# Slots 6 to 29 of a gated cross-attention block in another order: outputs turned by DMA, projection one slot later, tokens' low part on GpSimd

## The reference

```python
x = x + jnp.tanh(g_xattn[0]) * _L0_xattn_ref(_layernorm(x, axis=-1), ctx_768, mask, Wq, Wk, Wv, Wo)
x = x + jnp.tanh(g_ffn[0]) * _L0_ffn_ref(_layernorm(x, axis=-1), clip_x, clip_down, w_gate, w_up, w_down)
```

## Time and profile before

| | |
|---|---|
| median of 3 runs | 621.61 us (620.71 to 624.11) |
| the profiled execution | 621.71 us, span 619.9 us |
| busy in the span | PE 600.6, DVE 517.4, ACT 376.0, POOL 235.2 us |
| granted TensorE clock, mean | 0.991 |

### The profile page before, as it was taken

How to read it: one execution, slowest core, us unless ns; L and a number is a source line. 1 busy time by engine, 2 the same in 40 slices (tenths; PEclk the granted TensorE clock), 3 DMA queues, 4 the chain that set the end, 5 groups by cost and what they waited for, 6 DMA issues and landing times. The chain is left out here.

```text
span 619.9 us, 12094 instructions
## 1 busy us (share of the span) xinstructions
PE 600.6 (97%) x3706; PEld 448.7 (72%) x3727; DVE 517.4 (83%) x957; ACT 376.0 (61%) x484; POOL 235.2 (38%) x473
## 2 busy tenths in 40 slices
PE   8999999999999999999999886999999999899997
PEld 6799999999999999999899873444444444444544
DVE  6788899999999998999889857888888888866765
ACT  5554677877777777777774435555555553455653
POOL 6253454545454454445333112111011110067775
PEclk9999999999999999999999997999999999899999
DMA  8534885463434444634642000396653110199633
GB/s 310 174 116 121 197 192 106 82 112 80 109 81 100 89 92 92 126 81 91 124 103 59 16 1 10 75 252 226 205 158 87 35 34 1 45 369 396 242 117 120
DMA packets 118507, 77.89 MB, mean 126 GB/s; under 512 B 98211, under 2 KB 100669, under 8 KB 118461
## 3 DMA queue, kind: packets, MB, share of 16 engines
q1 hardware_dynamic: 113169, 60.51, 38.4%
q10 hardware_dynamic: 5292, 16.82, 7.6%
HBM read 32.48 MB, written 21.36 MB: 87 GB/s over the span
## 5 line engine op out<-in xcount | busy, mean ns | idle before, releaser
L1452 ACT ACTIVATE sb_silu<-ps_g,sb_sgu 128x512 f32<-128x512 f32 x88 | 60.5, 687 | 72.1 <-PE ps_g L1547 43.5
L1547 PE MATMUL ps_g<-sb_xqT,sb_wgu 128*128 128x512 bf16 x344 | 89.3, 379 | 1.0 <-DVE sb_xqT L1503 0.6
L1547 PE MATMUL ps_u<-sb_xqT,sb_wgu 128*128 128x512 bf16 x346 | 89.4, 379 | 0.3
L1518 DVE SCALAR_TENSOR_TENSOR sb_h<-ps_u,sb_sgu,sb_silu 128x512 f32<-128x512 f32 (+1 forms) x88 | 66.1, 751 | 19.8 <-PE ps_u L1547 18.9
L1069 PE MATMUL ps_q<-sb_xT_hi,sb_wq_hi 128*128 128x256 f32 x256 | 75.3, 294 | 0.9 <-DVE sb_xT_lo L764 0.6
L632 ACT ACTIVATE sb_prob<-sb_prob 128x616 f32<-128x616 f32 x64 | 45.6, 713 | 46.5 <-DVE sb_prob L797 46.5
L1628 POOL TENSOR_TENSOR sb_wgu<-sb_wgu,sb_x 128x512 f32<-128x512 f32 x31 | 53.3, 1721 | 53.7 <-DVE sb_wgu L1685 53.4
L1071 PE MATMUL ps_q<-sb_xT_hi,sb_wq_lo 128*128 128x256 f32 x256 | 72.4, 283 | 0.0
L1070 PE MATMUL ps_q<-sb_xT_lo,sb_wq_hi 128*128 128x256 f32 x256 | 72.3, 283 | 0.0
L1752 PE MATMUL ps_z<-sb_wdT,sb_hq 128*128 128x512 bf16 x324 | 71.3, 379 | 0.3
L1522 DVE TENSOR_REDUCE sb_hmax<-sb_h 128x1 f32<-128x512 f32 (+1 forms) x88 | 60.4, 686 | 7.6
(11 more groups left out here) (238 smaller groups left out, 1426.2 us busy)
## 6 DMA issues: line engine op xcount, KB each, us to landing
h_spill<-sb_h SPq DMA_DIRECT2D x4, 2816.0 KB, 9.5
sb_h<-h_spill ACTq DMA_DIRECT2D x16, 704.0 KB, 6.6
out_dram<-sb_wgu SPq DMA_DIRECT2D x31, 256.0 KB, 2.2
sb_x<-in_x_dram ACTq DMA_DIRECT2D x5, 1024.0 KB, 6.6
sb_w_in<-in_L_ffn_w_gate_dram SPq DMA_DIRECT2D x11, 256.0 KB, 2.7
sb_w_in<-in_L_ffn_w_up_dram SPq DMA_DIRECT2D x11, 256.0 KB, 2.6
sb_x<-in_x_dram SPq DMA_DIRECT2D x2, 1024.0 KB, 14.6
sb_x<-in_x_dram SPq DMA_DIRECT2D x2, 512.0 KB, 4.7
```

What stands on the lines that cost most here:

```text
L1452: act.activation(silu[(j * KI + i) % 2][:, :, :].rearrange("p t n -> p (t n)"), p_g[(j * KI + i) % 2][:, :], ACT.Silu, scale=sgu[:, i:i + ...
L1518: dve.scalar_tensor_tensor(steps_h, p_u[(j * KI + i) % 2][:, :, :], sgu[:, KI + i:KI + i + 1], silu[(j * KI + i) % 2][:, :, :], ALU.mult, ...
L1547: last = pe.matmul(banks[(j * KI + i) % 2][:, :], wgu[:, what, k, i * P:(i + 1) * P], xqT[j][:, k, :], start=(k == 0), stop=(k == KD - 1))
```

## The change

In slots 6 to 29 (`lagging`) and, for the parts that trail, 7 to 30 (`lagged`), each engine gets an order of its own:

- The outputs of tiles 4 to 27 are transposed by DMA. DVE writes `o_sb` as before, POOL splits it into planes (`out_split`, into the same buffer as the probabilities' planes), SP transposes back into `o_sb` (`outs_transposed`), ACT joins the planes (1024 half words) and casts the high part, DVE subtracts for the low part from the joined copy. `out_transpose` is gone for these tiles.
- TensorE projects tile n-3 right behind the first scores of tile n, and `outputs(n-1)` stands last in the slot.
- The low part of the tokens is computed by POOL (`x_low`), for tile n+3 in slot n. ACT's join of the tokens moves to the start of the slot, for tile n+3.
- DVE scales the second half of the outputs one slot later, and takes the weight rows' maximum and rounding at other places.
- `prob_transposed(n)` also waits for `out_part(n-2)`. Some semaphores are merged (t_ck into t_c) or renamed.

```diff
+LAG0 = 6
+OUT0, OUT1 = LAG0 - 2, NT - 4
...
+                o_u = o_sb[:, :].bitcast(U16)
+                o_pairs = o_u.rearrange("p (n two) -> p two n", two=2)
+                o_planes = o_u.rearrange("p (two n) -> p two n", two=2)
+                opl_planes = ppl_u[:, 0, 0:2 * D].rearrange("p (two n) -> p two n", two=2)
+                oT_pairs = ppl_u[:, 1, 0:2 * D].rearrange("p (n two) -> p two n", two=2)
+                oT_whole = ppl_u[:, 1, 0:2 * D].bitcast(F32).rearrange("p (k n) -> p k n", k=KD)
...
+                def lagging(n):
+
+                    return not isinstance(n, int) or LAG0 <= n < PROB1
+
+                def lagged(n):
+
+                    return not isinstance(n, int) or LAG0 < n <= PROB1
...
                         sp.wait_ge(a_p, 2 * n)
+                        if out_by_dma(n - 2):
+                            sp.wait_ge(v_olo, n - 1)
                         sp.dma_start_transpose(ppl_u[:, 1, :].rearrange("p (c n) -> p c n", n=P),
                                                ppl_u[:, 0, :]).then_inc(d_pT, 16)
+
+                    def outs_transposed(m):
+                        if out_by_dma(m):
+                            sp.wait_ge(g_opl, m - OUT0 + 1)
+                            sp.dma_start_transpose(o_u.rearrange("p (c n) -> p c n", n=P),
+                                                   ppl_u[:, 0, 0:2 * D]).then_inc(d_oT, 16)
 
...
                         rows_transposed(w - 2)
+                        outs_transposed(w - 3)
...
                     down_rows(0)
+                    outs_transposed(NW - 2)
                     planes_transposed(NW + 4)
                     prob_transposed(NW)
                     for r in range(KD):
+                        outs_transposed(WD0 + 2 * r - 1)
...
+                        if out_by_dma(n - 2):
+                            wait(pool, d_oT, 16 * (n - 1 - OUT0))
                         pool.tensor_tensor(carry[:, :], eps[:, :], minus[:, :], ALU.mult)
                         pool.tensor_copy(ppl_planes[:, :, 0:HW], prob_pairs).then_inc(g_ppl, 1)
+
+                    def out_split(m):
+
+                        wait(pool, v_o, 2 * m + 2)
+                        wait(pool, d_pT, 16 * (m + 2 - PROB0))
+                        pool.tensor_tensor(carry[:, :], eps[:, :], minus[:, :], ALU.mult)
+                        pool.tensor_copy(opl_planes, o_pairs).then_inc(g_opl, 1)
+
+                    def x_low(n, t):
+                        wait(pool, a_xhi, n + 1)
+                        wait(pool, x_lo_in, n)
+                        wait(pool, t_q, n - t % 2 - 2)
+                        cols = slice(t % 2 * P, (t % 2 + 1) * P)
+                        pool.tensor_tensor(xT_lo[t // 2][:, :, cols], xpl_T, xT_hi[t // 2][:, :, cols].bitcast(F32),
+                                           ALU.subtract).then_inc(x_lo_in, 1)
 
                     def deviation2(m):
...
+                        if lagging(n):
+                            out_split(n - 2)
+                        if lagged(n) and runs(n + 3, NT):
+                            x_low(n + 3, (t + 3) % 4)
...
+                    def out_high(m):
+                        wait(act, t_y, m)
+                        if out_by_dma(m):
+                            wait(act, d_oT, 16 * (m + 1 - OUT0))
+                            wait(act, a_p, 2 * m + 3)
+                            act.copy(oT_pairs, o_planes).then_inc(o_turned, 1)
+                            wait(act, o_turned, m + 1)
+                            act.copy(oT(m)[0], oT_whole).then_inc(a_ohi, 1)
+                        else:
+                            wait(act, o_turned, m + 1)
+                            act.copy(oT(m)[0], p_x[:, :, :]).then_inc(a_ohi, 1)
+
+                    def row_abs(m):
+                        wait(act, g_nb2, m + 1)
+                        wait(act, v_xmax, m + 1)
+                        if isinstance(m, int) and m + 4 >= PLANES_FREE:
+                            act.wait_ge(x_lo_in, NT)
+                        else:
+                            wait(act, v_x1, m + 2)
+                        act.activation(xabs(m), row(m), ACT.Abs, bias=nb2[:, span(m)],
+                                       scale=rs2[:, span(m)]).then_inc(a_abs, 1)
+
+                    def lagging_slot(n, t):
+
+
+                        if lagged(n) and runs(n + 3, NT):
+                            x_join(n + 3, (t + 3) % 4)
+                            if runs(n + 4, NT):
+                                normalise(n + 4, t + 4)
+                        exponential(n, 0)
+                        prob_join(n - 1)
+                        out_high(n - 2)
+                        row_abs(n - 4)
+                        prob_copy(n - 1, 1)
+                        if runs(n + 2, NT):
+                            q_part(n + 2, (t + 2) % 4)
+                        exponential(n, 1)
...
+                        whole = oT_whole if out_by_dma(m) else p_x[:, :, :]
+                        dve.tensor_tensor(o_lo, whole, o_hi.bitcast(F32), ALU.subtract).then_inc(v_olo, 1)
...
+                    def lagging_slot(n, t):
+                        m = n - 3
+                        if lagged(n):
+                            outputs_rec(n - 2, 1)
+                            outputs_norm(n - 2, 1)
+                        scores_max(n, 0)
+                        if runs(n, NW):
+                            wait(dve, d_w, 16 * n + 16)
+                            wait(dve, g_sc, n)
+                            dve.tensor_reduce(w_am[:, :], w_in[:, :], X, ALU.max, apply_absolute_value=True)\
+                               .then_inc(v_wam, 1)
+                        down_part(n, 0)
+                        if runs(n + 6, NT):
+                            wait(dve, v_st, n + 6)
+                            tokens_there(n + 6)
+                        scores_sub(n, t, 0)
+                        if runs(n + 6, NT):
+                            stats(n + 6)
+                        if runs(n, NW):
+                            wait(dve, v_wam, n + 1)
+                            wait(dve, v_wi8, n)
+                            dve.reciprocal(w_inv[:, :], w_am[:, :]).then_inc(v_winv, 1)
+                        wait(dve, t_y, m + 1)
+                        if runs(n + 6, NT):
+                            wait(dve, v_bn, n + 7)
+                            wait(dve, g_nb, n + 5)
+                        dve.tensor_tensor(row(m), y_full(m)[:, 0:D], row(m), ALU.add).then_inc(v_x1, 1)
+                        if runs(n + 6, NT):
+                            stats_end(n + 6, t)
+                        wait(dve, v_x1, m + 1)
+                        wait(dve, v_st2, m)
+                        if runs(n, NW):
+                            wait(dve, v_winv, n + 1)
+                            wait(dve, g_wbf, n)
+                            dve.tensor_scalar(w_i8[:, :], w_in[:, :], w_inv[:, :], QMAX, ALU.mult, ALU.mult)\
+                               .then_inc(v_wi8, 1)
+                        down_part(n, 1)
+                        dve.bn_stats(bn2[:, 0, :], row(m)).then_inc(v_bn2, 1)
+                        down_part(n, 2)
+                        down_scale(n)
+                        wait(dve, v_bn2, m + 1)
+                        wait(dve, g_nb2, m)
+                        scores_max(n, 1)
+                        dve.bn_aggr(mvt[:, :], bn2[:, 0, :]).then_inc(v_st2, 1)
+                        out_part(n - 2)
+                        scores_sub(n, t, 1)
+                        row_max(n - 4)
+                        if runs(n + 2, NT):
+                            q_part(n + 2, (t + 2) % 4)
+                        outputs_rec(n - 1, 0)
+                        outputs_norm(n - 1, 0)
...
 
-                        out_transpose(n - 2)
+                        if lagged(n):
+                            project(n - 3)
+                        if not out_by_dma(n - 2):
+                            out_transpose(n - 2)
                         prob_transpose(n - 1, 1)
                         if last_by_dma(n):
                             outputs(n - 1, 0)
                             outputs(n - 1, 1)
                             scores(n, t, 1)
                             project(n - 2)
+                            return
+                        if lagging(n):
+                            if runs(n + 2, NT):
+                                queries(n + 2, (t + 2) % 4, 0)
+                            scores(n, t, 1)
+                            if runs(n + 2, NT):
+                                queries(n + 2, (t + 2) % 4, 1)
+                            outputs(n - 1, 0)
+                            outputs(n - 1, 1)
                             return
                         for part in range(2):
```

More of the change, by code:

```diff
@@ L254, in flamingo_block @@
                 t_c = sem("t_c")
-                t_ck = sem("t_ck")
                 v_row = sem("v_row")
@@ L514, in deviation @@
                             wait(pool, a_xn, n)
```

(8 more changed lines are left out.)

53 lines of the change are left out of this document (38 added, 15 removed).

## The result

The changed kernel takes 687.67 us (median of 6 runs, 685.95 to 691.12) where the one before took 621.59 in the same series: a ratio of 1.106, 95% interval 1.102 to 1.109. I had predicted 662, range 634 to 674. The direction and the places were right, the size was not. The profiled execution took 691.12 us with a span of 689.3, the slowest of the six, so differences between profiles are a few us larger here than between medians.

What follows compares the result with a forecast made beforehand. TensorE set the 10.63 us slot before; waits through ACT, SP's queue and down-row loads would bind after. Slots 6 to 29 gain 37.1 us and slot 30 2.9: 621.7 + 40.0 = 662 us, range 634 to 674.

Steps and rivals of the forecast that it cites:

- What TensorE gets: Attention slots: output transposes leave TensorE, saving 0.44 us a slot, so TensorE alone needs 10.19 us.
- The loop through ACT: `outputs` waits for the late `prob_copy`, 8.80 us into the slot: 11.11 us a slot against 10.63.
- The loop through SP's queue: Slots 7 to 21: weight-row load queued behind the probabilities' transpose, which waits for `prob_copy`: 11.60 us a slot.
- The rows of the down weights: Row maximum waits for three loads: slot 22 takes 14.5 us, slots 24, 26 and 28 take 16.0 each.
- The sum: Slots 6 to 29 take 292.2 us against 255.1 (+37.1), slot 30 +2.9: 662 us in all.
- TensorE's clock: Half clock after idle in slots 22, 24, 26 and 28: about 2 us each, 670 us; not in the 662.
- rival 2: The clock falls in the four slots 22, 24, 26 and 28 as well: 670 us, chance 0.24.
- rival 6: Worse than the other cases: outputs' POOL copy, transpose and join arrive after ACT's join too; above 674 us, chance 0.08.
- 4 (TensorE stays the bound): Faster: 23 x 0.44 = 10.1 us less, 611.5 us, if `prob_copy` ends at 7.9 us; chance 0.08.

Runs made afterwards that it cites:

- e10: e7 plus VectorE's weight-row maximum behind the first score subtraction and the subtraction for the queries' low part moved to the next slot: 627.82 us (1.011).
- e3: The changed kernel with SyncE issuing the weight-row loads of slots 7 to 21 ahead of the probabilities' transpose: 681.85 us (1.094).
- e2: The changed kernel with ScalarE's copy of the probabilities moved right behind the join of the other half, ahead of the outputs' join: 663.29 us (1.066).
- e11: The changed kernel with one more ScalarE operation of 128x512 values ahead of the probabilities' copy in slots 6 to 29: 703.36 us (1.127).
- e1: The changed kernel with unread extra products on TensorE between queries and outputs in slots 6 to 29, to fill its gaps: 675.37 us (1.088).
- e5: The changed kernel with VectorE's maxima of the down rows (slots 22, 24, 26, 28) all behind the residual's statistics: 675.48 us (1.082).
- e4: The changed kernel with both the moves of e2 (ScalarE's copy) and e3 (SyncE's row loads): 658.71 us (1.059).
- e7: The changed kernel with the moves of e2, e3 and e5, and the joined outputs kept in the second half of the probabilities' own buffer: 638.25 us (1.024).
- e8: e7 with GpSimd computing the tokens' low part ahead of the split of the outputs: 664.13 us (1.064).
- e12: e10 with SyncE issuing the loads of the next down rows ahead of the two stores of the current ones: 635.87 us (1.024).

## Why the prediction was wrong

**What TensorE gets**: right in kind. With the waits mended (e10) a slot of 7 to 21 is 10.43 us against 10.58; 10.19 was predicted for TensorE alone, and it is busy 10.37 of the 10.43. So the 0.44 us shrink to about 0.2 of TensorE's time and 0.15 of the slot's. Why isn't shown: I have no separate run for it.

**The loop through ACT**: right. The run is 5.65 us for 5.62; the wait in slot 13 is 1.32 for 0.9; alone, at full clock (e3), the loop is 11.3 to 11.4 for 11.11. Moving the copy gave 24.4 us (e2), lengthening the run cost 15.7 (e11).

**The loop through SP's queue**: right, 11.83 us a slot for 11.60 with the clock back (e1), and 11.3 to 11.4 without it (e3).

**The rows of the down weights**: right, 14.50 for 14.5 in slot 22, 16.3 and 16.5 for 16.0 in two of the others (e1); taking the maxima later gave 12.2 us (e5). But the rest of what holds these slots, stores ahead of the outputs' way on GpSimd, had no term.

**The sum**: its terms cover 292.2 of the 321.6 us; slot 30 is 2.8 longer, 2.9 predicted. Of the 29.4 left over, 15.9 go when the gaps are filled (profiles: 321.6 and 305.7). The 13.5 that stay in e1 are slot 6 (14.86 for 11.11), slots 7 to 21 (+3.4), slots 22 to 28 even (+3.0) and 23 to 29 odd (+3.4).

**TensorE's clock** is the step that failed. The sum put it at nothing; I gave it 2 us in each of the four longest slots, and only in rival 2, against which I wrote "the gaps here are shorter" than the 4.64 us of the earlier trace rows. That didn't even fit my own numbers: 10.2 us of work in slots of 16.0 leave 5.8 us idle. In the profile the longest gap was 4.64 us as well, in slot 6; the clock fell within it and stood at half for some 10 us, most of them work (0.52 from 94.6 to 104.8, the gap ended at 96.33). Most gaps were shorter, and the clock still fell: behind 1.32 us in slot 13, and it was below 1.00 on average in 21 of the 24 slots. With the gaps filled 12.3 of the 25.7 us by which the median was missed went away (e1). The Trainium skill ("TensorE: Matmul & The Clock Gate", section "A second HAM failure mode: psum-queue depth-cycling") says that brief idle spells of TensorE that come back between groups can make its clock swing between both levels. This trace agrees in slots 13 to 19, where gaps of 1.28 to 1.45 us came back every second slot and the slots' clock was 0.87 to 0.97; slots 12 to 21 of e3, with 0.9 to 1.0 us in every slot at 1.00, show that they need not. I had read only the section on long gaps.

**Slot 6** was counted as an ordinary one, 11.11 us. It took 15.6: a transpose that shares its time with 1 MB of loads takes 6.6 us, and it stood ahead of `prob_copy` on ACT. With `prob_copy` ahead of it the slot took 11.6 (e2), with the same loads and a transpose that landed after 6.2 us. That was rival 6, "the outputs' own way (POOL copy, transpose, join) arrives after ACT's join too", in one slot. The measured time lies in this rival's region, above 674 us, which had a chance of 0.08, but its mechanism carries only some 4 us of it; the clock of rival 2, in far more slots than it named, carries the largest part.

**The rivals**: 4 (TensorE stays the bound) had this right, that only another order on ACT would give it. But more orders than ACT's had to change: SP's for the rows, DVE's for the down rows, the queries and a buffer. I had no term for the ring of the outputs, since in the changed kernel the ACT loop is longer and hides it. It showed in e4, and could have been added up from the order alone.

**Still open**: what decides whether a gap is followed by a fall of the clock (1.72, 1.25 and, in e4, 2.42 us were not, 1.28 was); how the clock's share and the waits' divide in the changed kernel beyond e1; which of the two rings of e7 is the longer; and why some loads took 4.3 us behind the transpose and others 2.9.

## What to carry to other kernels

- A gap on TensorE costs its own length, and sometimes as much again in clock: behind the 1.32 us of slot 13, 3 us at half clock cost 1.5. Behind other gaps of 1 to 2.4 us it cost nothing. Where a change makes a slot wait in every turn, give the clock a range in the sum, from nothing to the length of the wait in each turn, and fill the gaps as a test.
- A new step in a pipeline closes a ring over slots: add up its whole way (copy, issue, landing, join, cast, subtraction, next wait) and compare it with the period, also while something else still hides it. Here the rings were 11.0, 11.1 and 11.6 us long, and mending one showed the next.
- Before a transfer or an instruction is put first in a queue, name everything that then stands behind it. In e8 a wait of up to 0.9 us was to be mended, and the slots came out 1.2 us longer; in e12 waits of 0.8 to 1.7 us went, and slot 24 alone came out 4.7 us longer.

## What the runs showed of the hardware

- The clock stood at the lower level for 3 us, from some 2 us after a gap of 1.32 us had ended, while TensorE was working without a pause. A trace that is read for the wait alone doesn't show it: the slow matmuls stand elsewhere than the gap.
- Gaps of 1.72 us (slot 10), 1.25 us (slot 21) and, in e4, 2.42 us had no such stretch behind them, and neither had 0.9 to 1.0 us in each of ten slots in a row (e3).
- GpSimd's subtraction of 128x512 fp32 values took 1.27 to 1.30 us, less than the 1.72 of the addition in the earlier trace rows.
- A transpose of 1024 half words for each partition landed after 3.0 us, and after 6.6 us beside a 1 MB load from another queue. A load of 256 KB right behind the transpose of the probabilities took 2.9 to 4.3 us, where it took 2.4 to 3.4 in the kernel before, issued some 0.7 us later behind that transpose.
